# Hybrid attention block: one reduction over two banks, the first bank's mask as a product, transposes one slot later

## Chip, cores, metric

One core of a Trainium2 chip. The metric is the device time of one execution in microseconds.

## What is computed

An input of 8 sequences of 256 tokens with 128 channels goes through four layers, each as `x = x + layer(layernorm(x))`: a differential attention, a feed forward, a causal linear attention, and the same feed forward again. The change is in the first of them. Cut to what matters:

```
Q, K, V = (X @ W).reshape(B, N, 16, 16)          # 16 heads, 2 maps of width 8 in each
A1 = where(causal, Q1 K1^T / sqrt(8), -inf)
A2 = where(causal, Q2 K2^T / sqrt(8), -inf)
attn = softmax(A1) - lam * softmax(A2)
O = attn @ V
O = O / rms(O) * rms_scale * 0.2
x = x + O @ Wo
```

So each sequence has 32 maps of 256 x 256 scores with a causal mask, 256 maps in all, and the softmax subtracts the maximum of each row.

## The kernel before

The program has a first block (projections to Q and K, split into three bf16 parts each, and the composed weights of the feed forward) and a second one that holds the attention and all that follows. Every engine's order is written out by hand: a loop over *slots*, and in each slot each engine takes the piece of work that belongs to it, of units at different ages. Semaphores tie the engines together.

A *unit* is four maps; there are 64 units, four to a *group* of 16 maps, eight to a sequence. In its own slot a unit is scored (lag 0). Query rows 0 to 127 can only see keys 0 to 127, so their four maps of 128 x 128 fit in PSUM bank 0 (`S_BANK`, L1002). Query rows 128 to 255 see all 256 keys; they take banks 1 and 2, two maps of 128 x 256 in each (L1007). There is one set of these three banks, so a unit's scores wait until the unit before has had its row maxima taken from the same bank (`scores_wait`, semaphore `maxed`). The future keys are masked in two ways. In banks 1 and 2 PE adds a product of a bf16 identity and a bf16 matrix of -1e30 above the diagonal, 256 columns for each bank (`score_masks`, L1015), at the end of the slot's scores. In bank 0 VectorE does it: one instruction for each of the four maps adds the matrix `future` and takes the row maximum (L948), with an accumulator read after each. Banks 1 and 2 get one reduction each (L953). The maxima go to `rowmax`.

The rest of a unit's life, as lags in slots behind its scoring (L71, L72):

- 4 (`L_SHIFT`), once for a group: PE transposes `rowmax` (L1105), ScalarE makes the high part of the shift (L898), VectorE the low part (L914), and SP writes both as rows next to the queries (`store_shift`, L736).
- 6 (`L_EXP`): PE computes the scores once more, transposed and with the shift in them (L1039, L1044), into banks 3 and 4; ScalarE takes the exponentials (L824), GpSimd zeroes the future (L776). This is interleaved with the scores of the current unit in `both`.
- 8 (`L_PV`): PE multiplies with the values (L1081, L1085, bank 5 or 6), ScalarE copies the result (L842).
- 9 (`L_OT`): PE transposes it (L1127, bank 7), ScalarE copies it (L851).

Once for a sequence, counted from its first unit, follow the reciprocal of the denominators (16, VectorE L972), products and difference on GpSimd (16, 17), squares and their sum (19, ScalarE L868, VectorE L932), the inverse root (20), GpSimd's normalisation (21, L757), the transposes of the normalised output into bank 7 (`L_OPT` 21, L1139) with ScalarE's copy (L887), the output projection (`L_OPROJ` 22, L1157) with VectorE's residual (L923), and the statistics for the next layer norm (`L_STAT` 22, L281 to L289). The transposes of a sequence thus stand on PE at the end of slots 5, 13, 21 and so on, and the projection in the slot after.

In each slot PE's order is: bank 0 of the current unit with the first third of the shifted scores; values; rowmax transposes or the output projection where due; banks 1 and 2 with the other shifted scores; masks (L1015); output transposes (L1127); transposes of the normalised output (L1139) where due. VectorE's order is: bank 0's maxima; low part of the shift and residual where due; bank 1's; mean squares where due; bank 2's; reciprocal; statistics.

## Time and profile before

| | |
|---|---|
| median of 3 runs | 455.25 us (454.56 to 455.97) |
| profiled execution | 455.39 us |
| its span, first to last instruction | 453.3 us |
| mean granted TensorE clock | 0.944 |
| PE busy | 386.5 us, 85% |
| VectorE (DVE) busy | 293.9 us, 65% |
| ScalarE (ACT) busy | 257.0 us, 57% |
| GpSimd (POOL) busy | 203.2 us, 45% |

Shares of the span are averages over stages: the first block lasts to about 90 us, the scoring of the 64 units from 94 to 280 us, the end of the attention to about 300 us, and then come the feed forward, the linear attention and the second feed forward. In the rows, PE is a product, PEld the load of its stationary operand, and a time in brackets is how long the engine stood idle before the row and what ended that. Rows of the same line that follow closely are merged, with their number behind an x.

### The profile page before, as it was taken

How to read it: one execution, taken by the hardware profiler on the slowest of the kernel's cores; microseconds unless marked ns; L12 is line 12 of the kernel's file. 1: busy time of each engine (PE TensorE's matmuls, PEld its weight loads, DVE VectorE, ACT ScalarE, POOL GpSimd, SP SyncE). 2: the span in 40 equal slices, each digit the busy share in tenths (PEclk: the TensorE clock that was granted, in tenths of full speed). 3: DMA queues.
4: the chain of work that ended last, by engine and by line, in shares of the span. 5: the costliest groups of instructions: out<-in, count | busy, mean ns of one | idle time of the engine just before them, and what ended most of it. 6: DMA issues, size and time to landing. Idle time of an engine off the chain costs nothing.

```text
span 453.3 us, 10148 instructions
## 1 busy us (share of the span) xinstructions
PE 386.5 (85%) x3380; PEld 244.5 (54%) x3380; DVE 293.9 (65%) x1019; ACT 257.0 (57%) x631; POOL 203.2 (45%) x324
## 2 busy tenths in 40 slices
PE   0799689769999888979799798888688999999996
PEld 0566479623455544545455454444475666555674
DVE  6576454169899797989989797110142789999201
ACT  3333134203688777877878686847667433444832
POOL 5223224001558475675848485733001788773000
PEclk9999799955899999999999999956999999999999
DMA  8889969953555434242544400000000000000011
GB/s 205 251 269 309 260 143 235 217 86 46 81 82 82 74 60 76 36 89 35 87 59 75 72 3 3 4 1 0 0 2 1 1 0 2 0 0 2 0 48 46
DMA packets 47347, 34.51 MB, mean 76 GB/s; under 512 B 20032, under 2 KB 41664, under 8 KB 47296
## 3 DMA queue, kind: packets, MB, share of 16 engines
q1 hardware_dynamic: 47296, 33.86, 35.8%
q8 instruction: 28, 0.46, 0.5%
q14 instruction: 23, 0.19, 0.2%
HBM read 25.20 MB, written 8.39 MB: 74 GB/s over the span
## 4 chain that ended last, share of the span: by engine, by line
PE 31%; DVE 26%; issue 9%; ACT 8%; POOL 4%; DMA 1%; DVEq 0%; POOLq 0%; SPq 0%
DVE ps L948 7%; DVE arena L953 7%; PE ps L1258 5%; PE ps L1249 3%; PE ps L1081 3%; PE ps L1461 3%; PE ps L1007 3%; DVE arena L1392 3%; DVE arena L948 2%; PE ps L1157 2%; ACT arena L1202 2%; ACT arena L824 2%; POOL arena L757 2%; PE ps L1002 2%; DVE arena L1405 2%
## 5 line engine op out<-in xcount | busy, mean ns | idle before, releaser
L776 POOL TENSOR_SCALAR_AFFINE_SELECT arena<-arena 128x256 f32<-128x256 f32 (+1 forms) x192 | 90.3, 482 | 97.8 <-ACT arena L824 93.8
L824 ACT ACTIVATE arena<-ps 128x512 f32<-128x512 f32 x192 | 109.5, 604 | 26.0 <-PE ps L1039 25.5
L953 DVE TENSOR_REDUCE arena<-ps 128x2 f32<-128x512 f32 x128 | 82.9, 686 | 6.5 <-PE ps L1015 6.0
L948 DVE CUSTOM_DVE_ANT_0 ps<-ps,future 128x128 f32<-128x128 f32 x256 | 66.4, 321 | 11.9 <-PE ps L1002 11.5
L1039 PE MATMUL ps<-stacks 50*128 50x256 bf16 x256 | 51.4, 281 | 1.2 <-ACT arena L824 1.1
L1333 POOL TENSOR_TENSOR arena<-arena 128x1024 f32<-128x1024 f32 x16 | 34.2, 2134 | 32.6 <-DVE arena L1418 32.1
L1007 PE MATMUL ps<-stacks 48*128 48x256 bf16 x256 | 45.5, 288 | 0.9 <-ACT arena L824 0.5
L391 POOL TENSOR_TENSOR qk_parts_sb<-qk_rest,qk_parts_sb 128x512 bf16<-128x512 f32 x16 | 19.1, 1209 | 51.2 <-DVE qk_parts_sb L491 51.2
L1081 PE MATMUL ps<-arena 128*17 128x256 f32 x512 | 41.4, 396 | 0.0
L1002 PE MATMUL ps<-stacks 48*128 48x128 bf16 x256 | 26.7, 228 | 16.8 <-DVE ps L906 6.1
L948 DVE DVE_READ_ACCUMULATOR2_ANT arena<- 128x1 f32 x256 | 36.3, 142 | 0.0
L1461 PE MATMUL ps<-arena,upto 128*128 128x384 f32 x96 | 36.0, 487 | 0.0
L1002 PEld LDWEIGHTS ps<-stacks 48*128 48x128 bf16 x256 | 15.7, 98 | 31.1 <-issue 17.6
L1258 PE MATMUL ps<-w,arena 128*128 128x128 f32 x256 | 30.3, 276 | 1.8 <-ACT arena L1225 1.3
L1258 PEld LDWEIGHTS ps<-w,arena 128*128 128x128 f32 x256 | 29.3, 192 | 3.8 <-ACT arena L1225 2.0
L1249 PE MATMUL ps<-arena,w 128*128 128x512 f32 x64 | 30.6, 627 | 0.3 <-DVE arena L1392 0.3
L1007 PEld LDWEIGHTS ps<-stacks 48*128 48x128 bf16 x256 | 17.8, 96 | 22.6 <-issue 10.7
L1231 DVE TENSOR_TENSOR xs<-ps,xs 128x512 f32<-128x512 f32 x8 | 5.5, 690 | 34.1 <-PE ps L1258 34.1
L1127 PE MATMUL ps<-ident,arena 128*128 128x128 f32 x128 | 26.3, 288 | 1.4 <-issue 0.6
L1015 PE MATMUL ps<-future_bf,ident_bf 128*128 128x256 bf16 x128 | 26.8, 294 | 0.0
L1085 PE MATMUL ps<-arena 128*17 128x128 f32 x512 | 26.4, 279 | 0.0
L1044 PE MATMUL ps<-stacks 50*128 50x128 bf16 x256 | 25.6, 222 | 0.0
(129 smaller groups left out, 750.6 us busy)
## 6 DMA issues: line engine op xcount, KB each, us to landing
stacks<-qk_parts SPq DMA_DIRECT2D x96, 128.0 KB, 4.6
qk_parts<-qk_parts_sb SPq DMA_DIRECT2D x16, 384.0 KB, 4.1
arena<-in_L_ffn_fc_B_dram SPq DMA_DIRECT2D x4, 1024.0 KB, 7.3
arena<-in_L_ffn_fc_A_dram SPq DMA_DIRECT2D x16, 256.0 KB, 4.7
xs<-in_L_attn_a_X_dram SPq DMA_DIRECT2D x4, 256.0 KB, 4.0
qk_parts<-qk_parts_sb SPq DMA_DIRECT2D x8, 128.0 KB, 4.4
stacks<-arena SPq DMA_DIRECT2D x64, 4.0 KB
out_dram<-xs SPq DMA_DIRECT2D x4, 256.0 KB, 2.3
```

The costliest lines, as they stand in the source:

```text
L776: nc.gpsimd.affine_select(out=diag, in_=diag, compare_op=ALU.is_ge, fill=0.0, base=0, pattern=[[0, 2 if s < 2 else UMAPS], [1, P]], channe ...
L824: nc.scalar.activation(probs[:, r, s, :], ps[:, bank, :], ACT.Exp, scale=SCALE).then_inc(exp_done, 1)
L948: last = nc.vector.tensor_tensor_reduce(out=block, in0=block, in1=future[:], scale=1.0, scalar=LOWEST, op0=ALU.add, op1=ALU.max, accum_out ...
L953: last = nc.vector.tensor_reduce(out=rowmax[:, gs, 1, at:at + 2], in_=ps[:, bank, :].rearrange("p (m k) -> p m k", m=2), axis=AX, op=ALU.max)
L1002: last = nc.tensor.matmul(bank[:, m * P:(m + 1) * P], q[:, m0 + m, 0:P], k[:, m0 + m, 0:P], start=True, stop=True)
L1007: nc.tensor.matmul(bank[:, m * SEQ:(m + 1) * SEQ], q[:, m0 + 2 * s - 2 + m, P:SEQ], k[:, m0 + 2 * s - 2 + m, :], start=(m == 0), stop=Fals ...
L1039: last = nc.tensor.matmul(bank[:, m * SEQ:(m + 1) * SEQ], k[:, m0 + 2 * s + m, 0:P], q[:, m0 + 2 * s + m, :], start=True, stop=True)
L1081: nc.tensor.matmul(ps[32 * m:32 * m + DV + 1, O_BANK + r, 0:SEQ], vaug[:, v, 0, head, :], probs[:, p, m // 2, m % 2 * SEQ:m % 2 * SEQ + SE ...
L1249: nc.tensor.matmul(ps[:, 2 + c, :], w1[:, c * P:(c + 1) * P], f_xnT[:, k % 2, :], start=True, stop=True).then_inc(S["up"], 1)
L1258: last = nc.tensor.matmul(ps[:, 6 + k % 2, t * D:(t + 1) * D], hT[:, k % 2, c, t * P:(t + 1) * P], w2[:, c, :], start=(c == 0), stop=(c == ...
L1333: nc.gpsimd.tensor_tensor(kv[:, w, t, 0:DH, :].rearrange("p e (h d) -> p e h d", d=DH), kh.unsqueeze(1).to_broadcast([P, DH, HEADS, DH]), ...
L1461: last = nc.tensor.matmul(bank, upto[:], rows, start=True, stop=(t == 0))
```

## The change

Bank 0 is masked as the other two are: `score_masks` gets a third product, of 512 columns, ahead of the two of 256, so bank 0's scores are left open (`stop=False`) and its semaphore count comes from that product. VectorE takes one reduction over bank 0 (four maps) and one over banks 1 and 2 together (four maps); the second waits for all three banks and counts two on `maxed`. `future` goes, and `future_bf` holds four copies. The transposes of the normalised output, the output projection and the statistics come one slot later each. In the diff, `...` marks what is left out.

```
-L_DEN, L_DIFF, L_SQ, L_MS, L_ROOT, L_NORM, L_OPT, L_OPROJ, L_STAT = 16, 17, 19, 19, 20, 21, 21, 22, 22
+L_DEN, L_DIFF, L_SQ, L_MS, L_ROOT, L_NORM, L_OPT, L_OPROJ, L_STAT = 16, 17, 19, 19, 20, 21, 22, 23, 23
...
-                nc.gpsimd.memset(future[:], 0.0)
...
-                                        base=0, pattern=[[0, 2], [-1, P]], channel_multiplier=1)
-                nc.gpsimd.affine_select(out=future[:], in_=future[:], compare_op=ALU.is_ge, fill=NEG,
-                                        base=0, pattern=[[-1, P]], channel_multiplier=1).then_inc(consts, 1)
+                                        base=0, pattern=[[0, UMAPS], [-1, P]], channel_multiplier=1)\
+                    .then_inc(consts, 1)
...
-                    for s in range(BANKS_U):
-                        bank = S_BANK + s
-                        dve.wait_ge(scored, BANKS_U * n + s + 1)
-                        if s == 0:
-
-                            carry_wait(dve, tick_dve)
-                            for m in range(UMAPS):
-                                block = ps[:, bank, m * P:(m + 1) * P]
-                                at = UMAPS * uu + m
-                                last = nc.vector.tensor_tensor_reduce(
-                                    out=block, in0=block, in1=future[:], scale=1.0, scalar=LOWEST, op0=ALU.add,
-                                    op1=ALU.max, accum_out=rowmax[:, gs, 0, at:at + 1])
-                        else:
-                            at = UMAPS * uu + 2 * s - 2
-                            last = nc.vector.tensor_reduce(
-                                out=rowmax[:, gs, 1, at:at + 2], in_=ps[:, bank, :].rearrange("p (m k) -> p m k", m=2),
-                                axis=AX, op=ALU.max)
-                        last.then_inc(maxed, 1)
-                        if s == 0:
-                            shift_low(it, j)
-                            residual(it, j)
-                        if s == 1:
-                            mean_squares(it, j)
+                    dve.wait_ge(scored, BANKS_U * n + 1)
+                    nc.vector.tensor_reduce(
+                        out=rowmax[:, gs, 0, UMAPS * uu:UMAPS * (uu + 1)],
+                        in_=ps[:, S_BANK, :].rearrange("p (m k) -> p m k", m=UMAPS),
+                        axis=AX, op=ALU.max).then_inc(maxed, 1)
+                    shift_low(it, j)
+                    residual(it, j)
+                    dve.wait_ge(scored, BANKS_U * (n + 1))
+                    nc.vector.tensor_reduce(
+                        out=rowmax[:, gs, 1, UMAPS * uu:UMAPS * (uu + 1)],
+                        in_=ps[:, S_BANK + 1:S_BANK + 3, :].rearrange("p b (m k) -> p (b m) k", m=2),
+                        axis=AX, op=ALU.max).then_inc(maxed, 2)
+                    mean_squares(it, j)
...
-                    last = nc.tensor.matmul(bank[:, m * P:(m + 1) * P], q[:, m0 + m, 0:P],
-                                            k[:, m0 + m, 0:P], start=True, stop=True)
-                    if m == UMAPS - 1:
-                        last.then_inc(scored, 1)
+                    nc.tensor.matmul(bank[:, m * P:(m + 1) * P], q[:, m0 + m, 0:P],
+                                     k[:, m0 + m, 0:P], start=(m == 0), stop=False, skip_group_check=True)
...
+                    nc.tensor.matmul(ps[:, S_BANK, :], ident_bf[:], future_bf[:].rearrange("p m k -> p (m k)"),
+                                     start=False, stop=True, skip_group_check=True).then_inc(scored, 1)
```

The order on PE from the scores of bank 2 to the next unit's bank 0, in a plain slot. Before (L1007 scores of banks 1 and 2, L1044 shifted scores, L1015 masks, L1127 output transposes, L1002 scores of bank 0):

```order
L1007 MATMUL ps<-stacks 128x256 [waits exp_done,maxed]
L1044 MATMUL ps<-stacks 128x128
L1007 MATMUL ps<-stacks 128x256
L1044 MATMUL ps<-stacks 128x128 x3
L1015 MATMUL ps<-future_bf,ident_bf 128x2x128 x2
L1127 MATMUL ps<-ident,arena 128x128 [waits o_copied,ot_copied]
L1127 MATMUL ps<-ident,arena 128x128
L1002 MATMUL ps<-stacks 128x128 [waits exp_done,maxed]
```

and with the change, where the same lines are L992, L1031, L1002, L1114 and L989, and L998 is the new mask:

```order
L992 MATMUL ps<-stacks 128x256 [waits exp_done,maxed]
L1031 MATMUL ps<-stacks 128x128
L992 MATMUL ps<-stacks 128x256
L1031 MATMUL ps<-stacks 128x128 x3
L998 MATMUL ps<-future_bf,ident_bf 128x512
L1002 MATMUL ps<-future_bf,ident_bf 128x2x128 x2
L1114 MATMUL ps<-ident,arena 128x128 [waits o_copied,ot_copied]
L1114 MATMUL ps<-ident,arena 128x128
L989 MATMUL ps<-stacks 128x128 [waits exp_done,maxed]
```

The last writer of bank 0 now stands four instructions ahead of the next unit's first scores in it, where before it stood at the slot's beginning.

VectorE in a slot with a shift, before (L948 masked maxima, named ISA, with the reads of the accumulator; L914 low part of the shift):

```order
L948 ISA ps,arena<-ps,future 128x128
L948 ISA arena 128x1
L914 SCALAR_TENSOR_TENSOR arena<-ps,arena 16x256
L953 TENSOR_REDUCE arena<-ps 128x2 x2
L972 RECIPROCAL arena<-arena 128x64
```

and now (L937 bank 0, L911 the low part, L944 banks 1 and 2, L959 the reciprocal):

```order
L937 TENSOR_REDUCE arena<-ps 128x4 [waits scored]
L911 SCALAR_TENSOR_TENSOR arena<-ps,arena 16x256 [waits shift_hi]
L944 TENSOR_REDUCE arena<-ps 128x4 [waits scored]
L959 RECIPROCAL arena<-arena 128x64 [waits post,o_copied]
L937 TENSOR_REDUCE arena<-ps 128x4 [waits scored]
L944 TENSOR_REDUCE arena<-ps 128x4 [waits scored]
```

The low part keeps its place behind bank 0's maximum, which itself now follows the mask product.

PE around the transposes of the normalised output, before (L1139 the transposes, L1157 the projection of the next slot):

```order
L1127 MATMUL ps<-ident,arena 128x128
L1139 MATMUL ps<-ident,arena 128x128 [waits resid_done,o_copied,normed]
L1139 MATMUL ps<-ident,arena 128x128 x3
L1002 MATMUL ps<-stacks 128x128 [waits exp_done,shift_in20,maxed]
L1039 MATMUL ps<-stacks 128x256
```

and now (L1126 the transposes, L1144 the projection):

```order
L1114 MATMUL ps<-ident,arena 128x128
L1126 MATMUL ps<-ident,arena 128x128 [waits resid_done,o_copied,normed]
L1126 MATMUL ps<-ident,arena 128x128 x3
L989 MATMUL ps<-stacks 128x128 [waits exp_done,maxed]
L1026 MATMUL ps<-stacks 128x256
```

The neighbours are the same; the whole piece stands one slot later, so that the scores behind it wait for no shift rows.

## Rows read from the trace of the kernel before

**Rows 1.** The page, part 4: shares of the chain that ended last
```profile
PE 31%; DVE 26%; issue 9%; ACT 8%; POOL 4%; DMA 1%; DVEq 0%; POOLq 0%; SPq 0%
```

**Rows 2.** Stretches: stretch, its us, busy PE, PEld, DVE, ACT, POOL, PEclk, DMA
```profile
94.00:114.00 20.00, 18.22 (x98) 6.85 (x98) 18.04 (x81) 4.24 (x8) 2.18 (x5) 0.50 0.47 70
...
118.00:276.00 158.00, 137.66 (x2003) 80.14 (x1998) 138.37 (x587) 124.24 (x310) 102.43 (x191) 1.00 0.41 64
...
292.00:304.00 12.00, 10.12 (x80) 5.58 (x80) 0.69 (x1) 7.61 (x25) 5.83 (x12) 0.59 0.01 1
```

**Rows 3.** Timeline, a plain slot: start us, us, engine, line, operation
```profile
212.20 0.23 PE L1002 MATMUL ps<-stacks 48*128 48x128 bf16 x1
...
213.30 0.28 PE L1007 MATMUL ps<-stacks 48*128 48x256 bf16 x1
...
213.39 0.27 DVE L948 CUSTOM_DVE_ANT_0 ps<-ps,future 128x128 f32<-128x128 f32 x1
...
213.85 0.39 PE L1015 MATMUL ps<-future_bf,ident_bf 128*128 128x256 bf16 x2
...
214.32 1.28 DVE L953 TENSOR_REDUCE arena<-ps 128x2 f32<-128x512 f32 x2
214.52 0.23 PE L1002 MATMUL ps<-stacks 48*128 48x128 bf16 x1
```

**Rows 4.** Timeline, a slot with rowmax transposes, ahead of rows 3
```profile
209.44 0.21 PE L1002 MATMUL ps<-stacks 48*128 48x128 bf16 x1 [0.80 <-DVE arena L948]
...
210.85 0.28 PE L1007 MATMUL ps<-stacks 48*128 48x256 bf16 x1
...
211.36 0.41 DVE L914 SCALAR_TENSOR_TENSOR arena<-ps,arena 16x256 bf16<-16x256 f32 x1
...
211.83 0.44 PE L1127 MATMUL ps<-ident,arena 128*128 128x128 f32 x2
```

**Rows 5.** Timeline, the end of slot 37 and slot 38 to its bank 1
```profile
200.28 0.39 PE L1015 MATMUL ps<-future_bf,ident_bf 128*128 128x256 bf16 x2
...
200.60 1.29 DVE L953 TENSOR_REDUCE arena<-ps 128x2 f32<-128x512 f32 x2 [0.35 <-PE ps L1015]
...
201.29 0.30 ACT L851 COPY arena<-ps 128x136 f32<-128x136 f32 x1
...
202.31 0.66 PE L1139 MATMUL ps<-ident,arena 128*128 128x128 f32 x4 [1.42 <-POOL arena L757]
...
202.90 0.23 PE L1002 MATMUL ps<-stacks 48*128 48x128 bf16 x1
...
205.09 0.28 PE L1007 MATMUL ps<-stacks 48*128 48x256 bf16 x1
```

**Rows 6.** Timeline, PE: first scores of units 24, 46, 56 and 63
```profile
159.80 0.21 PE L1002 MATMUL ps<-stacks 48*128 48x128 bf16 x1 [0.80 <-DVE arena L948]
...
227.20 0.23 PE L1002 MATMUL ps<-stacks 48*128 48x128 bf16 x1
...
258.04 0.21 PE L1002 MATMUL ps<-stacks 48*128 48x128 bf16 x1 [0.80 <-DVE arena L948]
...
279.16 0.21 PE L1002 MATMUL ps<-stacks 48*128 48x128 bf16 x1
```

**Rows 7.** The page, part 5: the masked maxima
```profile
L948 DVE CUSTOM_DVE_ANT_0 ps<-ps,future 128x128 f32<-128x128 f32 x256 | 66.4, 321 | 11.9 <-PE ps L1002 11.5
```

**Rows 8.** One line, L1405: durations ns min/median/max, first and last start, forms
```profile
L1405 DVE TENSOR_REDUCE arena<-arena x16: 1353/1353/1354, 357.5 to 416.9; 128x144 f32<-128x1152 f32 x16
```

**Rows 9.** Timeline, units 4 and 8 (last row), at the low clock
```profile
105.33 1.03 PE L1007 MATMUL ps<-stacks 48*128 48x256 bf16 x4
...
106.29 0.61 PE L1015 MATMUL ps<-future_bf,ident_bf 128*128 128x256 bf16 x2
...
106.72 1.29 DVE L953 TENSOR_REDUCE arena<-ps 128x2 f32<-128x512 f32 x2 [0.47 <-PE ps L1015]
...
117.14 0.39 PE L1015 MATMUL ps<-future_bf,ident_bf 128*128 128x256 bf16 x2
```

More of the change, by code:

```diff
@@ L112, in hybrid_kernel @@
         ident_bf = sb("ident_bf", [P, P], BF16)
-        future = sb("future", [P, P])
-        future_bf = sb("future_bf", [P, 2, P], BF16)
+        future_bf = sb("future_bf", [P, UMAPS, P], BF16)
         upto = sb("upto", [P, P])
@@ L1015, in score_masks @@
                         nc.tensor.matmul(bank.rearrange("p (m k) -> p m k", m=2)[:, :, P:SEQ], ident_bf[:],
-                                         future_bf[:], start=False, stop=True,
+                                         future_bf[:, 0:2], start=False, stop=True,
                                          skip_group_check=True).then_inc(scored, 1)
```

## The prediction

> **What bounds the kernel now.** I read the chain of waits first [rows 1]: no engine carries most of it, so the stages have to be looked at one by one. The table of stretches [rows 2] shows that the change falls into one stretch, 94 to 280 us, in which the 64 units of four maps are scored. From 118 to 276 us PE is busy 137.7 of 158 us and VectorE 138.4: two engines in balance, and neither wait is long. In the timeline of a plain slot [rows 3] the slot begins at 212.20 and the next at 214.52, so it takes 2.3 us. In it VectorE's four masked maxima take 0.93 (213.39 to 214.32) and the two reductions 1.28, together 2.2. What matters is how they interlock. Bank 0's maxima run while PE weighs values and scores banks 1 and 2; the reductions of banks 1 and 2 run while PE does its masks, its transposes and the next unit's bank 0. The slot is full on both engines and neither waits for a round trip.
>
> From here m is the start of a slot's first mask product (L1015), B the start of its bank 0 scores (L1002), b the start of its bank 1 scores (L1007). A plain slot [rows 3]: B to b 1.10 (212.20 to 213.30), b to m 0.55, m to the next B 0.67 or less.
>
> The other slots of a sequence (eight slots) carry extras: a slot with rowmax transposes has B to b 1.41, 0.31 more, and VectorE's low half of the shift (L914, 0.41) [rows 4]; one waits for GpSimd's normalisation before its transposes, which start 2.03 after m at 202.31, and the next has the output projection, B to b 2.19 (202.90 to 205.09) [rows 5]. Eight slots repeat in 24.30 us (202.90 [rows 5] to 227.20 [rows 6]).
>
> **The change part by part.** *VectorE.* Off go 4 masked maxima a unit, 256 of 321 ns with their 256 accumulator reads [rows 7]; one reduction of 512 elements comes, 0.69 as L953's. Two reductions of 512 become one of 1024. No row has it; the nearest is L1405's, 1152 elements in 1353 ns from SBUF [rows 8]. Between 0.69 for 512 and 1.35 for 1152 it is 1.04 ns an element, so 1.22 us; bounds 1.15 and 1.40. VectorE's plain slot falls from 2.2 to 0.60 (the spacing of back-to-back reductions: 1.28 less 0.69) and 1.22, 1.8 us. Alone that would be a gain of 0.4 us a slot.
>
> *PE.* One product of 512 columns a unit. Two of 256 columns (L1015) take 0.39 together where one (L1007) takes 0.28 [rows 3], so 256 columns are 0.11 and 512 are 0.22. The Trainium skill, "TensorE: Matmul & The Clock Gate", section "Back-to-back issue gap", gives some 131 ns for a product of 512 columns in a stream of weight loads and products; by it the sum below would be 0.09 times 64, some 6 us, smaller. Nothing below uses it.
>
> *The wait that comes.* Bank 0 is now complete only after this mask, which PE issues at the end of the slot, and the next thing that PE wants after masks and output transposes is the same bank 0 (it waits for the maximum of it). So mask, maximum, next scores are one after another, and everything behind is queued: values, banks 1 and 2, and again the mask. Its length: mask to reduction is 0.32 for 256 columns (200.28 to 200.60 [rows 5]), 0.11 more for 512, 0.43; the reduction 0.69; VectorE to PE 0.06 (L914 ends 211.77, L1127 starts 211.83 [rows 4]). Next B = m + 1.18, where PE would be free at about 0.67 + 0.22. The wide reduction ends at m + 0.43 + 0.60 + 1.22 = m + 2.25, so b = m + 2.31, PE itself being there at 2.28. Then 0.55 to the next mask: **a plain slot takes 2.86 instead of 2.3.**
>
> *Slots with extras.* The low half of the shift and the residual (VectorE 0.41, 0.42) stand behind the bank 0 reduction, and PE waits for each before its output transposes: it ends at m + 0.43 + 0.60 + 0.41 = 1.44, transposes at 1.50, next B 0.35 later at m + 1.85 (211.83 to 212.20 is 0.37 [rows 4]). Such a slot takes 1.85 + 1.10 + 0.55 = 3.50. Into a slot with rowmax transposes: 2.31 + 0.31 + 0.55 = 3.17; out of the projection's slot and into one of these: 1.85 + 1.41 + 0.55 = 3.81. *The later transposes* gain: normalisation is done by then, and what they wait for is ScalarE's copy of the output transposes (L851 ends 1.31 after m [rows 5], 1.45 with what precedes it now); with 0.59 to B it is m + 2.04, where before it was 2.62. But the projection's 2.19 follows: 2.04 + 2.19 + 0.55 = 4.78. Mean squares, reciprocal and statistics on VectorE fall into its new idle time and cost nothing; if the slot became short again they would be back on the chain, some 2.2 us a sequence. GpSimd loses a memset and a select in the first block, under DMA: nothing. SP's queue keeps its order. A shift's rows land up to 3.2 us after the low half; now PE comes for them 3.2 us after it as well, so 0 to 0.3 us 14 times: 0 taken, 4 in the range.
>
> *Sum.* A sequence: 3 x 2.86 + 3.17 + 2 x 3.50 + 4.78 + 3.81 = 27.34, against 24.30: 3 us each.
> - Units 0 to 8 run at half clock (granted 0.50 in 94 to 114 us [rows 2]): mask to reduction 0.43 (106.29 to 106.72) and 0.21 for the columns, 1.82, 0.06, b to m 0.96 [rows 9], 3.48 against a plain 2.3: 8 slots, 9.4, with the extras of units 4 and 8 **10**.
> - From unit 8's mask (117.14 [rows 9]) to unit 24 (159.80 [rows 6]) 42.66 now; then 4 x 3.50 + 7 x 2.86 + 3 x 3.17 + 4.78 + 1.85 = 50.16: **7.5**.
> - Units 24 to 56, 159.80 to 258.04 [rows 6], 98.24 now; 4 x 27.34 = 109.4: **11.1**.
> - Units 56 to 63, 21.12 now (to 279.16 [rows 6]); 1.41 + 0.55 + 2 x 3.50 + 3 x 2.86 + 3.17 + 2.04 = 22.75: **1.6**.
> - The last projection, 1.08, moves behind unit 63: **1.1**. After it the order of the tail is as before: nothing.
>
> Together 31.3 us. The profiled execution took 455.39 us (0.14 above the median of 455.25): 486.7, **487 us**.
>
> **The rivals.** *Faster: PE is the bound.* If the round trip from mask to next B cost no more than PE's own work (0.22 + 0.67), VectorE's relief would show: eight slots of 2.30 + 0.22, two times 0.31, 1.08 for the projection and 0.59 for the transposes, 22.5 us a sequence, 1.8 less, some 14 us in all: 441 us. For it: VectorE and PE are both nearly full now, and the 1.4 us wait of the later transposes really goes. Against: the reduction alone is 0.69, and both waits are in the program. The sign turns where the round trip is 0.38 shorter than 1.18, that is a reduction of 0.3 us. Chance 5 in 100.
> *No difference*, the two effects cancelling within 0.3%, about what a measurement of this kernel can tell from no change: the round trip would be 0.8 long. 2 in 100.
> *The clock stays low.* The granted clock was 0.50 (1.2 GHz) up to 114 us while PE was busy 18.2 of 20 us in the records, was 1.00 from 118 on, and fell again, to a mean of 0.59, in 292 to 304 us when PE was thinner [rows 2]. With 0.3 to 0.9 us of waiting in every slot PE may be granted 1.2 GHz later, or lose 2.4 GHz between. At half clock a slot has 0.64 + 0.69 + 0.06 to B, up to twice 1.10 to b and 0.96 to m, 4.55 instead of 2.86: if the rise comes 16 slots later that is 27 us (514 us), if never, in some 55 slots, 93 (580 us). Against: now waits of 1.42 us [rows 5] come in each sequence and 118 to 276 us has 1.00 throughout. The same page of the Trainium skill, Part 1, says that the low clock is the default and activity releases it; by it this case is the likelier the thinner PE's work becomes. Chance 10 in 100.
> *The change does less than it says*: the reduction over two banks costs two instructions' time. 1.29 for 1.22 delays b by 0.07: 4 us, inside the range.
>
> **How the numbers follow.** My forecast has 83 in 100 and is itself slower. Its bounds: every step of the loop 0.1 shorter is 6 us less; the mask at half its price 6; a clock that rises a few units sooner 3. Upwards: the wide reduction at 1.40, 0.18 in some 50 slots, 9; the shift's rows 4; clock up a few slots later 5. Not all at once: 477 to 500, and into the clock's case up to 506. Slower 0.93, same 0.02, faster 0.05.
>
> **What would show it.** Right: slots of 2.86 and 3.50, a sequence of 27 us; PE idle before L989 some 0.3 to 0.9 us in nearly every slot, put down to VectorE's L937; VectorE busy some 60 us less, with over 0.8 us idle before L937 in a slot; L1126 no longer waiting for GpSimd but for ScalarE's copy, if anything. Wrong: L989 starting within 0.9 us after L998, slots of 2.5 us, or a clock row of 0.50 beyond 135 us.

## The result, and the profile after

The changed kernel takes 483.64 us, the median of 4 runs (481.34 to 485.84), beside 455.61 (454.56 to 459.62) for the kernel before: a ratio of 1.060 (95% interval 1.055 to 1.065), 28.0 us more. 487 was forecast. Ratios, here and below, leave out executions more than 1.5% above the fastest of the same kernel, which ran at a lower clock; medians and ranges hold all of them. Its profiled execution took 483.22 us, with a span of 481.5 and a mean granted clock of 0.946.

The page of the changed kernel: busy times, shares of the chain that ended last, and the groups (busy us, mean ns | idle before, what ended it).

```profile
PE 395.7 (82%) x3444; PEld 250.1 (52%) x3444; DVE 264.0 (55%) x507; ACT 261.5 (54%) x631; POOL 203.6 (42%) x322
...
PE 48%; DVE 14%; issue 9%; ACT 7%; POOL 2%; DVEq 0%; POOLq 0%
...
L937 DVE TENSOR_REDUCE arena<-ps 128x4 f32<-128x512 f32 x64 | 44.3, 692 | 87.8 <-PE ps L998 87.8
L944 DVE TENSOR_REDUCE arena<-ps 128x4 f32<-128x1024 f32 x64 | 77.5, 1212 | 0.0
...
L989 PE MATMUL ps<-stacks 48*128 48x128 bf16 x256 | 27.3, 232 | 22.5 <-DVE arena L937 11.6
...
L1114 PE MATMUL ps<-ident,arena 128*128 128x128 f32 x128 | 26.0, 285 | 18.3 <-DVE arena L911 11.9
```

VectorE is busy 30 us less than before and now stands idle 87.8 us ahead of bank 0's maximum, all of it for the mask product L998. PE waits in its turn for that maximum (L989) and for the low part of the shift behind it (L1114). The chain's share of VectorE fell from 26% [rows 1] to 14%, though the kernel got slower: the chain now goes through PE, the mask and back. By the page alone VectorE would seem to have been relieved and PE to have become the bound. The slots tell more.

Timeline of the changed kernel, two plain slots.

```profile
239.66 0.23 PE L989 MATMUL ps<-stacks 48*128 48x128 bf16 x1 [0.35 <-DVE arena L937]
...
240.79 0.28 PE L992 MATMUL ps<-stacks 48*128 48x256 bf16 x1
...
241.34 0.39 PE L998 MATMUL ps<-future_bf,ident_bf 128*128 128x512 bf16 x1
...
241.77 0.69 DVE L937 TENSOR_REDUCE arena<-ps 128x4 f32<-128x512 f32 x1 [1.03 <-PE ps L998]
...
242.38 1.22 DVE L944 TENSOR_REDUCE arena<-ps 128x4 f32<-128x1024 f32 x1
...
242.52 0.23 PE L989 MATMUL ps<-stacks 48*128 48x128 bf16 x1 [0.35 <-DVE arena L937]
...
243.65 0.28 PE L992 MATMUL ps<-stacks 48*128 48x256 bf16 x1
```

The loop reads off directly: mask product at 241.34, reduction 0.43 later, 0.69 long, the next bank 0 scores 0.06 behind its end, at 242.52. B to b is 1.13, b to m 0.55 (the prediction's letters: m the first mask, B bank 0's scores, b bank 1's). A plain slot takes 2.86 us, where [rows 3] have 2.3.

A slot that has the low part of the shift, from its mask to the next slot's start, same view:

```profile
234.97 0.39 PE L998 MATMUL ps<-future_bf,ident_bf 128*128 128x512 bf16 x1
...
235.40 0.69 DVE L937 TENSOR_REDUCE arena<-ps 128x4 f32<-128x512 f32 x1 [0.71 <-PE ps L998]
...
236.00 0.40 DVE L911 SCALAR_TENSOR_TENSOR arena<-ps,arena 16x256 bf16<-16x256 f32 x1
...
236.46 0.44 PE L1114 MATMUL ps<-ident,arena 128*128 128x128 f32 x2 [0.89 <-DVE arena L911]
...
236.83 0.23 PE L989 MATMUL ps<-stacks 48*128 48x128 bf16 x1
```

From mask to the next B it is 1.86 here, and PE stands 0.89 us before its output transposes.

The starts of units 0, 8, 24, 32, 40, 56 and 63 in the changed kernel, same view:

```profile
94.26 0.61 PE L989 MATMUL ps<-stacks 48*128 48x128 bf16 x4 [7.38 <-DVE ps L903]
...
122.37 0.26 PE L989 MATMUL ps<-stacks 48*128 48x128 bf16 x1 [0.40 <-issue]
...
178.11 0.23 PE L989 MATMUL ps<-stacks 48*128 48x128 bf16 x1
...
205.56 0.23 PE L989 MATMUL ps<-stacks 48*128 48x128 bf16 x1
...
233.00 0.23 PE L989 MATMUL ps<-stacks 48*128 48x128 bf16 x1
...
288.57 0.23 PE L989 MATMUL ps<-stacks 48*128 48x128 bf16 x1
...
311.39 0.23 PE L989 MATMUL ps<-stacks 48*128 48x128 bf16 x1
```

Before, unit 0 started at 94.69, 0.4 us later, and unit 8 at 114.09. The kernel before reaches unit 24 at 159.80 [rows 6], so 18.3 us are lost by then. Units 24 to 56 take 110.46 against 98.24, 12.2 more; units 56 to 63 22.82 against 21.12, 1.7 more. A sequence is 27.44 (205.56 to 233.00); the next one is 28.12, by one slot of 3.52 for 2.82, and the two around them 27.45. What follows unit 63's start is 4.0 us shorter: 481.5 less 311.39 is 170.1, and 453.3 less 279.16 [rows 6] is 174.1. With unit 0's start that makes 28.2 us of span.

Stretches of the changed kernel (us, busy PE, PEld, DVE, ACT, POOL, then the granted clock):

```profile
94.00:134.00 40.00, 32.44 (x216) 14.53 (x217) 19.13 (x24) 10.01 (x21) 6.20 (x13) 0.52 0.34 52
134.00:320.00 186.00, 152.81 (x2111) 88.55 (x2108) 116.64 (x171) 133.83 (x319) 104.40 (x194) 1.00 0.34 51
320.00:334.00 14.00, 11.59 (x142) 5.82 (x144) 1.35 (x4) 12.04 (x36) 11.38 (x20) 1.00 0.01 3
```

The clock rose only behind 132 us (granted 0.50 in 130 to 132, 0.91 in 132 to 134), where before it stood at 1.00 from 118 on [rows 2]. Behind unit 63 it was the other way: 2.4 GHz nearly throughout (mean 0.99 from 312 to 481 us), where before it was granted 0.59 between 292 and 304 us [rows 2] and 0.95 from 280 to 453.

### The profile page after: what moved, and what is told of

It is laid out like the page before. It is cut to its first block, busy times and chain, and to the rows that moved or that the text cites. A ratio compares the mean times of both kernels' runs of the same rounds, so it can differ in the third digit from the quotient of the medians.

```text
span 481.5 us, 9761 instructions
## 1 busy us (share of the span) xinstructions
PE 395.7 (82%) x3444; PEld 250.1 (52%) x3444; DVE 264.0 (55%) x507; ACT 261.5 (54%) x631; POOL 203.6 (42%) x322
## 4 chain that ended last, share of the span: by engine, by line
PE 48%; DVE 14%; issue 9%; ACT 7%; POOL 2%; DVEq 0%; POOLq 0%
PE ps L1068 7%; PE ps L992 7%; PE ps L1245 5%; PE ps L998 5%; DVE arena L937 5%; PE ps L989 3%; PE ps L1448 3%; PE ps L1072 3%; DVE arena L1379 2%; PE ps L1114 2%; PE ps L1236 2%; ACT arena L1189 2%; DVE arena L944 2%; PE ps L1026 2%; DVE arena L1392 1%
## 5 line engine op out<-in xcount | busy, mean ns | idle before, releaser
L773 POOL TENSOR_SCALAR_AFFINE_SELECT arena<-arena 128x256 f32<-128x256 f32 (+1 forms) x192 | 90.6, 482 | 125.8 <-ACT arena L821 121.5
L821 ACT ACTIVATE arena<-ps 128x512 f32<-128x512 f32 x192 | 107.9, 597 | 43.2 <-PE ps L1026 41.0
L937 DVE TENSOR_REDUCE arena<-ps 128x4 f32<-128x512 f32 x64 | 44.3, 692 | 87.8 <-PE ps L998 87.8
L944 DVE TENSOR_REDUCE arena<-ps 128x4 f32<-128x1024 f32 x64 | 77.5, 1212 | 0.0
L992 PE MATMUL ps<-stacks 48*128 48x256 bf16 x256 | 43.4, 293 | 3.5 <-DVE arena L944 3.5
L989 PE MATMUL ps<-stacks 48*128 48x128 bf16 x256 | 27.3, 232 | 22.5 <-DVE arena L937 11.6
L1114 PE MATMUL ps<-ident,arena 128*128 128x128 f32 x128 | 26.0, 285 | 18.3 <-DVE arena L911 11.9
L989 PEld LDWEIGHTS ps<-stacks 48*128 48x128 bf16 x256 | 15.6, 99 | 37.9 <-DVE arena L937 19.7
L1245 PE MATMUL ps<-w,arena 128*128 128x128 f32 x256 | 31.9, 286 | 1.8 <-ACT arena L1212 1.3
L1245 PEld LDWEIGHTS ps<-w,arena 128*128 128x128 f32 x256 | 30.9, 201 | 3.8 <-ACT arena L1212 2.0
L992 PEld LDWEIGHTS ps<-stacks 48*128 48x128 bf16 x256 | 20.1, 99 | 20.9 <-DVE arena L944 9.6
L1236 PE MATMUL ps<-arena,w 128*128 128x512 f32 x64 | 28.8, 595 | 0.3 <-DVE arena L1379 0.3
L1114 PEld LDWEIGHTS ps<-ident,arena 128*128 128x128 f32 x128 | 14.8, 142 | 25.1 <-DVE arena L911 15.7
L998 PE MATMUL ps<-future_bf,ident_bf 128*128 128x512 bf16 x64 | 27.1, 424 | 0.0
L1002 PE MATMUL ps<-future_bf,ident_bf 128*128 128x256 bf16 x128 | 26.9, 296 | 0.0
L1031 PE MATMUL ps<-stacks 50*128 50x128 bf16 x256 | 25.6, 222 | 0.0
```

The source lines that it names most:

```text
L773: nc.gpsimd.affine_select(out=diag, in_=diag, compare_op=ALU.is_ge, fill=0.0, base=0, pattern=[[0, 2 if s < 2 else UMAPS], [1, P]], channe ...
L821: nc.scalar.activation(probs[:, r, s, :], ps[:, bank, :], ACT.Exp, scale=SCALE).then_inc(exp_done, 1)
L937: nc.vector.tensor_reduce(out=rowmax[:, gs, 0, UMAPS * uu:UMAPS * (uu + 1)], in_=ps[:, S_BANK, :].rearrange("p (m k) -> p m k", m=UMAPS), ...
L944: nc.vector.tensor_reduce(out=rowmax[:, gs, 1, UMAPS * uu:UMAPS * (uu + 1)], in_=ps[:, S_BANK + 1:S_BANK + 3, :].rearrange("p b (m k) -> p ...
L989: nc.tensor.matmul(bank[:, m * P:(m + 1) * P], q[:, m0 + m, 0:P], k[:, m0 + m, 0:P], start=(m == 0), stop=False, skip_group_check=True)
L992: nc.tensor.matmul(bank[:, m * SEQ:(m + 1) * SEQ], q[:, m0 + 2 * s - 2 + m, P:SEQ], k[:, m0 + 2 * s - 2 + m, :], start=(m == 0), stop=Fals ...
```

## The experiments

The kernel before ran beside each set, at medians of 456.55 (e3 to e6), 457.54 (e1, e2, e7, e8) and 455.65 us (f1 to f4); ratios are to it, with 95% intervals. In the edits `...` marks what is left out. Since the end of the program moves with the clock, the one profiled execution of each is also cut at first scores, in us: the start of unit 0, four stretches between starts of units, from unit 63's start to the end (after), and from unit 0 to 63. It is one execution each, and a spell at the low clock falls where it falls: two of f1's sequences between units 24 and 56 are 24.8 long and the other two 23.3, which alone is 3 us.

| | start | units 0-8 | 8-24 | 24-56 | 56-63 | after | 0 to 63 |
|---|---|---|---|---|---|---|---|
| before | 94.7 | 19.4 | 45.7 | 98.2 | 21.1 | 174.1 | 184.5 |
| changed | 94.3 | 28.1 | 55.7 | 110.5 | 22.8 | 170.1 | 217.1 |
| e3 | 92.4 | 23.9 | 47.8 | 99.8 | 21.2 | 169.9 | 192.7 |
| e6 | 92.6 | 31.5 | 58.5 | 115.9 | 24.1 | 174.2 | 230.0 |
| e4 | 92.6 | 26.4 | 52.5 | 107.3 | 22.2 | 170.7 | 208.3 |
| e5 | 90.6 | 28.1 | 54.9 | 112.4 | 25.2 | 172.2 | 220.6 |
| e1 | 93.3 | 19.4 | 44.8 | 96.4 | 20.8 | 170.0 | 181.4 |
| e2 | 93.7 | 23.2 | 47.8 | 99.7 | 21.3 | 177.3 | 192.0 |
| e7 | 94.8 | 23.2 | 45.0 | 96.6 | 20.3 | 170.2 | 185.1 |
| f1 | 94.2 | 16.5 | 45.5 | 96.2 | 19.9 | 168.9 | 178.0 |
| f2 | 96.1 | 21.4 | 47.8 | 100.3 | 22.1 | 171.8 | 191.6 |
| f3 | 93.4 | 16.5 | 45.9 | 93.7 | 20.0 | 168.8 | 176.0 |
| f4 | 95.7 | 16.5 | 43.5 | 91.9 | 19.6 | 168.9 | 171.5 |

Three kernels first take the change apart at its suspected place: the round trip through bank 0.

**e3_mask_early.** The same product, issued right behind bank 0's scores.

```
-                    nc.tensor.matmul(ps[:, S_BANK, :], ident_bf[:], future_bf[:]...).then_inc(scored, 1)   # in score_masks
+                    nc.tensor.matmul(ps[:, S_BANK, :], ident_bf[:], future_bf[:]...).then_inc(scored, 1)   # in both(), after bank 0
```

> The changed kernel with one move: bank 0's mask product stands right behind bank 0's scores at the slot's beginning, and not at its end. Same work on every engine. Theory (the round trip mask, maximum, next scores at the slot's end is what costs): the maximum now runs beside the values, PE waits for it no longer, a plain slot falls from 2.86 to 2.45 to 2.5 us, a sequence from 27.4 to about 23, and the kernel takes 446 us (440 to 452), less than before the change. Rival A (the product's own time on PE, or the wide reduction, costs): nothing is gained, 478 to 486 us.

Measured: 458.75 us (456.56 to 462.5), ratio 1.009 [1.004, 1.014]. Moving one instruction takes back 24.9 of the 28 us, so the loss is a matter of where the product stands. But 446 was expected and it did not go below the kernel before: that half missed. Timeline of this kernel, a plain slot:

```profile
219.88 0.21 PE L989 MATMUL ps<-stacks 48*128 48x128 bf16 x1
...
220.89 0.68 DVE L937 TENSOR_REDUCE arena<-ps 128x4 f32<-128x512 f32 x1
...
221.30 0.28 PE L992 MATMUL ps<-stacks 48*128 48x256 bf16 x1
...
221.74 1.08 ACT L821 ACTIVATE arena<-ps 128x512 f32<-128x512 f32 x2 [0.57 <-PE ps L1024]
...
221.85 0.39 PE L1000 MATMUL ps<-future_bf,ident_bf 128*128 128x256 bf16 x2
...
222.48 0.21 PE L989 MATMUL ps<-stacks 48*128 48x128 bf16 x1
```

No wait stands before L989, and the slot still takes 2.60. B to b is 1.42 for 1.10 [rows 3], b to m 0.55 as there, m to B 0.63: here the product costs PE 0.32 us and not the 0.22 that it adds between the masks. PE's own order fills the slot, but f3 below shows that a second loop gives the same 2.60.

**e6_mask_last.** Bank 0's product behind the two others, and its maximum waits for all three.

```
-                    dve.wait_ge(scored, BANKS_U * n + 1)
+                    dve.wait_ge(scored, BANKS_U * (n + 1))
```

> The changed kernel with the three masks in the other order: banks 1 and 2 first, bank 0 last, and the bank 0 maximum waits for all three. Same work, but bank 0 is complete 0.22 us later. Theory: every slot gets 0.2 us longer, 64 slots, 12 to 14 us: 496 us (492 to 500). Rival A: the product costs the same wherever it stands among the masks, so 482 to 486 us.

Measured: 498.06 us (494.89 to 502.52), ratio 1.091 [1.081, 1.102]: 14.4 us over the changed kernel, as expected. Some 13 of it are in units 0 to 63; what follows is 4 us longer and unit 0 starts 1.7 earlier, so the nearness of 14.4 to 64 times 0.22 is in part chance. Timeline, end of a plain slot:

```profile
189.67 0.23 PE L989 MATMUL ps<-stacks 48*128 48x128 bf16 x1 [0.57 <-DVE arena L937]
...
191.35 0.39 PE L1000 MATMUL ps<-future_bf,ident_bf 128*128 128x256 bf16 x2
...
192.00 0.69 DVE L937 TENSOR_REDUCE arena<-ps 128x4 f32<-128x512 f32 x1 [1.25 <-PE ps L1000]
...
192.75 0.23 PE L989 MATMUL ps<-stacks 48*128 48x128 bf16 x1 [0.57 <-DVE arena L937]
```

The slot grew from 2.86 to 3.08, the 0.22 by which the mask is later: the loop from mask to maximum to scores is closed. In a steady sequence seven slots of eight grow by that much, and the one with the late transposes stays at 3.75. The amount of work is the changed kernel's own.

**e4_no_product.** The product is dropped, and bank 0's count comes from bank 1's mask, so the wait stays. Row maxima of bank 0 are taken over all of its keys.

```
-                    nc.tensor.matmul(ps[:, S_BANK, :], ident_bf[:], future_bf[:]...).then_inc(scored, 1)
...
-                                          skip_group_check=True).then_inc(scored, 1)
+                                          skip_group_check=True).then_inc(scored, s)
```

> The changed kernel without the product of 512 columns; the count for bank 0 comes from the first of the two masks that remain, so the maximum still starts at the slot's end. Bank 0's mask is left out of the row maxima. Theory: only 0.11 to 0.2 us a slot is saved (PE's columns, and the maximum starts 0.32 after the first mask instead of 0.43), so 472 to 477 us, still some 20 us slower than before the change. Rival A (the product's own time): back to 455 to 462 us.

Measured: 475.7 us (473.36 to 477.19), ratio 1.046 [1.036, 1.056], as expected: 7.9 us back, and the other 20 stay as long as the wait stays where it is. Timeline, a plain slot from its mask:

```profile
203.55 0.39 PE L1000 MATMUL ps<-future_bf,ident_bf 128*128 128x256 bf16 x2
...
203.88 0.69 DVE L937 TENSOR_REDUCE arena<-ps 128x4 f32<-128x512 f32 x1 [0.81 <-PE ps L1000]
...
204.62 0.23 PE L989 MATMUL ps<-stacks 48*128 48x128 bf16 x1 [0.46 <-DVE arena L937]
```

Even the 7.9 is not the product's own time on PE, which still waits 0.46 before the scores. It is the maximum, which starts 0.33 behind the mask and not 0.43; a plain slot is 2.72.

**e5_transposes_back.** The changed kernel with the transposes where they were.

```
-... L_OPT, L_OPROJ, L_STAT = 16, 17, 19, 19, 20, 21, 22, 23, 23
+... L_OPT, L_OPROJ, L_STAT = 16, 17, 19, 19, 20, 21, 21, 22, 22
```

> The changed kernel with the transposes, the projection and the statistics back in their old slots (21, 22, 22). Theory: PE waits for GpSimd's normalisation again, which ends about 2.1 us after the first mask of the slot where ScalarE's copy ends at 1.4: 0.6 to 0.7 us a sequence, 4 to 6 us, 488 to 490 us. Rival B (the later transposes are what costs): 470 us or less.

Measured: 490.7 us (485.2 to 495.0), ratio 1.069 [1.056, 1.082], 7.1 us over the changed kernel by the medians, but only 3.2 by the executions that the ratio rests on (485.2 and 488.4), and 3.5 in units 0 to 63 (a sequence 28.10 for 27.45); 4 to 6 were expected. Timeline:

```profile
221.76 0.66 PE L1126 MATMUL ps<-ident,arena 128*128 128x128 f32 x4 [1.30 <-POOL arena L754]
```

The wait for GpSimd's normalisation, as in [rows 5], is back: 20.5 us in all before L1126, where the changed kernel has 1.8 and the kernel before 21.3.

**e1_later_only.** The kernel before with nothing but the later lags: the same line, the other way.

> The kernel before with one part of the change: transposes, projection and statistics one slot later. Theory: PE waits for ScalarE's copy instead of GpSimd's normalisation, 0.65 us less for each of 8 sequences, and nothing new stands in the way since bank 0's maxima still run at the slot's beginning: 450 us (448 to 454). Rival B (the later pieces collide with something else): 455 or more.

Measured: 448.27 us (445.56 to 453.09), ratio 0.989 [0.981, 0.997]. The median is 9.3 us under that of before, yet units 0 to 63 are only 3.1 us shorter (181.4 for 184.5), and a sequence is 24.10 for 24.30. Much of the rest stands in the clock: before's own 17 runs of this set go from 449.42 us at a mean clock of 0.962 to 462.45 at 0.922, and e1's from 445.56 at 0.958. At like clocks (before 450.19 at 0.958) it is 4.6. The ratio says some 5 us. So by its own waits this part gains 0.65 us a steady sequence with the new masking (e5) but only 0.20 with the old; the rest of the 3.1 comes from single longer slots of the kernel before, one of them 3.46 for 2.3. In these profiles the stretch after unit 63 is another 2 to 4 shorter (174.1 to 170.0 here, 172.2 to 170.1 from e5 to the changed kernel).

**e2_wide_only.** The kernel before with one reduction over banks 1 and 2 and the mean squares behind it, masked maxima kept.

```
-                        dve.wait_ge(scored, BANKS_U * n + s + 1)
...
+                    dve.wait_ge(scored, BANKS_U * (n + 1))
+                    nc.vector.tensor_reduce(
+                        out=rowmax[:, gs, 1, UMAPS * uu:UMAPS * (uu + 1)],
+                        in_=ps[:, S_BANK + 1:S_BANK + 3, :].rearrange("p b (m k) -> p (b m) k", m=2),
+                        axis=AX, op=ALU.max).then_inc(maxed, 2)
```

> The kernel before with one part of the change: one reduction over banks 1 and 2 instead of two, bank 0 with VectorE's masked maxima as before. Theory: VectorE is relieved of some 0.06 us a slot, and bank 1's maximum is known 0.5 us later, which PE does not miss because the values stand between: no difference, 455 us (453 to 458). Rival C (the later count for bank 1 holds PE): 460 or more.

Measured: 465.32 us (463.48 to 467.4), ratio 1.028 [1.022, 1.035]. The expectation missed by 10 us, and rival C's 460 or more came. Timeline, a slot at the low clock:

```profile
98.61 0.60 PE L996 MATMUL ps<-stacks 48*128 48x128 bf16 x4
98.80 1.23 DVE L951 TENSOR_REDUCE arena<-ps 128x4 f32<-128x1024 f32 x1 [0.73 <-PE ps L1009]
...
100.08 1.03 PE L1001 MATMUL ps<-stacks 48*128 48x256 bf16 x4 [0.86 <-DVE arena L951]
...
101.04 0.61 PE L1009 MATMUL ps<-future_bf,ident_bf 128*128 128x256 bf16 x2
...
101.58 0.61 PE L996 MATMUL ps<-stacks 48*128 48x128 bf16 x4
```

The wide reduction makes a loop of its own: it starts only after bank 2's mask, and holds bank 1 until its end. Scores 0.96, mask to its start 0.73, 1.23 and 0.05 make 2.97 a slot, where the kernel before needs 2.3. From unit 0 to unit 8 that is 23.2 us against 19.4. Units 0 to 63 lose 7.5 in all, and 3.1 are lost behind them, where the clock was 0.65 from 300 to 330 us. All six runs had a mean clock of 0.919 to 0.930, so this goes with the edit; by what path isn't shown.

So far: e3 shows the round trip, but also that without it the masks on PE gain nothing over e1, which keeps them on VectorE (192.7 against 181.4 us for units 0 to 63). The next six look for what holds the slot when VectorE does not.

**e7_early_no_product.** e3 without the product; bank 0's mask is left out of the row maxima.

```
-                        nc.tensor.matmul(ps[:, S_BANK, :], ident_bf[:], future_bf[:]...).then_inc(scored, 1)   # in both()
...
+                    if m == UMAPS - 1:
+                        last.then_inc(scored, 1)
```

> The kernel with the early mask of bank 0 (458.75 us), without that product: bank 0's mask is left out of the row maxima, and the maximum follows the scores. Its timeline shows a plain slot of 2.60, in which scores and product take 0.64 where the scores alone took 0.32. Theory (once the round trip is gone PE's own work is the bound, and the product costs 0.3 us of it): a plain slot of 2.28, 64 x 0.3 = 20 us less, 440 us (436 to 446). Rival D (ScalarE or another engine is the bound at 2.5 us a slot): 452 or more.

Measured: 451.33 us (447.83 to 453.4), ratio 0.995 [0.990, 1.000]: 7.4 us under e3, well short of what was expected. It is also e4 with bank 0's count raised by its last scores and not by the mask at the slot's end, the same work for PE and VectorE: 475.7 to 451.3, and 208.3 to 185.1 for units 0 to 63. That is the round trip by itself. The plain slots stop at 2.3 to 2.4, though VectorE has 0.4 us a slot less to do than before and PE as much. Against e1, which has the same lags and VectorE's masks, units 24 to 56 take 96.6 for 96.4: relieving VectorE gains nothing there (a steady sequence is 23.70 for 24.10, but two of the four are 24.6).

**e8_no_masks.** As e7, and banks 1 and 2 without masks in the row maxima too (the exponentials are still masked, so the shift is a maximum over all keys, and the softmax divides it out).

```
-                for s in range(1, BANKS_U):
-                    nc.tensor.matmul(bank..., ident_bf[:], future_bf[:, 0:2], ...).then_inc(scored, 1)
+                return
```

> As the one before, and also without the masks of banks 1 and 2 in the row maxima. The shift is then the maximum over all keys, which the softmax cancels; the exponentials are masked afterwards as always. Theory: PE's slot loses 0.22 to 0.33 more and falls to 2.0, and ScalarE, whose three exponentials and two copies take some 2.3 us a slot, becomes the bound: a gain of at most 0.1 us a slot in plain slots and the full one in the others, 433 us (427 to 440). Rival E (PE's waits between slots stay): the same time as without bank 0's product.

Measured: 448.27 us (443.67 to 454.29), ratio 0.988 [0.980, 0.996]; missed by 15 us. The two masks are gone from PE, some 0.22 a slot, and plain slots are still 2.30. (Its profiled execution took 454.29, 6 above the median, so it isn't in the table.)

**f1_no_masks_two.** e8 with the two separate reductions of the kernel before.

> The kernel without masks in the row maxima (448.27 us), with one reduction each for banks 1 and 2 again instead of the wide one. Theory (the wide reduction makes a round trip of its own while the clock is low: in units 2 to 8 of the wide-reduction kernel a slot takes 2.97 us instead of 2.3): those slots shrink, 3 to 6 us less, 444 us (440 to 447). Rival: the wide reduction is not at fault there, no change, 448 or more.

Measured: 445.76 us (442.0 to 447.9), ratio 0.978 [0.972, 0.984], 2.5 us under e8 and inside what was expected, though the two intervals overlap. The slots are clearer: at the low clock plain ones fall to 1.80, and units 0 to 8 take 16.5 us for e8's 19.3, the wide reduction's price again.

**f2_early_two.** e3 with the two separate reductions; all masks kept.

> The kernel with bank 0's mask product behind bank 0's scores (458.75 us), with one reduction each for banks 1 and 2. Theory: the units at the low clock lose 0.5 us each, 4 to 6 us, 453 us (450 to 456); the later slots stay at 2.60, which PE's own work sets. Rival: 458 or more.

Measured: 458.59 us (456.67 to 461.94), ratio 1.009 [1.005, 1.013], as e3: missed. Units 0 to 8 are 2.5 us shorter, but units 24 to 63 1.4 and what follows 2.0 longer. The wide reduction is thus not what keeps e3 above e1 at the full clock; the product's 0.32 is, as e7 shows.

**f3_copy_on_dve.** f1 with the copy of the weighted values moved from ScalarE to VectorE.

```
-                    nc.scalar.copy(ot_sb[:, r, :], ps[:, O_BANK + r, 0:SEQ]).then_inc(ot_copied, 1)
+                    nc.vector.tensor_copy(ot_sb[:, r, :], ps[:, O_BANK + r, 0:SEQ]).then_inc(ot_copied, 1)
```

> The first kernel of this group with the copy of the weighted values (0.38 us a slot) moved from ScalarE to VectorE, which has the time now. It tells apart why plain slots stop at 2.30 whatever VectorE and PE are spared. Theory F (a round trip: the second exponential 0.60, 0.15 to PE's next bank 0 scores, 1.10 to the scores of bank 1, 0.44 to the next second exponential, 2.29 in all): the copy is not on it, no gain, within 3 us of the first kernel. Rival G (ScalarE's throughput, 2.0 to 2.3 us of work a slot): 10 to 15 us less.

Measured: 438.55 us (436.39 to 439.94), ratio 0.962 [0.957, 0.967], 7.2 us under f1: between the 3 at most of theory F and the 10 to 15 of rival G, so the time decides nothing and the slots have to. Timeline, a plain slot:

```profile
208.01 0.21 PE L991 MATMUL ps<-stacks 48*128 48x128 bf16 x1 [0.22 <-ACT arena L821]
...
209.11 0.28 PE L996 MATMUL ps<-stacks 48*128 48x256 bf16 x1
...
209.57 1.08 ACT L821 ACTIVATE arena<-ps 128x512 f32<-128x512 f32 x2 [0.47 <-PE ps L1024]
...
210.31 0.21 PE L991 MATMUL ps<-stacks 48*128 48x128 bf16 x1 [0.22 <-ACT arena L821]
```

PE and ScalarE both have gaps, so neither is full, and ScalarE has 0.4 us a slot less to do than in f1; still it takes 2.30. The legs of theory F's round trip add up to it: the first exponential of the pair (209.57) runs 0.60, to 210.17, and frees the bank that the next slot writes first; PE starts 0.14 later; B to b is 1.10; 0.46 after b the next pair starts. 0.60 + 0.14 + 1.10 + 0.46 = 2.30. e3's slot fits it too: 0.60 + 0.14 + 1.42 + 0.44 = 2.60. Its product stood between B and b, a leg of this loop as well as a part of PE's own work, so e3 alone cannot tell the two apart. The 7.2 us did not come from the slots: a steady sequence is 23.4 here and 23.3 in f1 (the slot with the late transposes 3.58 for 4.13, but others longer). The profiled executions differ by 2.9, of which 2.5 between units 24 and 56, where the clock was 1.00 from 156 to 250 us here and 0.96 in f1, which has slots of 4.5 to 5.0 in there. The rest is in executions without a profile: f3's six had mean clocks of 0.952 to 0.959, f1's 0.931 to 0.953, and f1's two at 0.950 and 0.953 took 442.85 and 442.0. So the clock explains the better part, and some 3 us at like clocks stay open.

**f4_split_values.** f1, with the second half of the values' products moved behind bank 1's scores, which shortens B to b.

```
-                    for t in range(TPS):
-                        weigh_values(it, j, t)
+                    weigh_values(it, j, 0)
...
+                if live(unit(it, j, L_PV), UNITS):
+                    weigh_values(it, j, 1)
```

> The first kernel of this group with the products with the values split on PE: the first half (L1081's) stays ahead of the scores of bank 1, the second half (L1085's) goes behind them. The same work. Theory F: the round trip of the second exponential loses the second half, 0.2 to 0.33 us, plain slots fall from 2.30 to 2.05 and the slots with more ScalarE work gain less: 8 to 15 us less than the first kernel, 434 us (429 to 440). Rival G (ScalarE's throughput): less than 3 us.

Measured: 437.98 us (435.13 to 445.96), ratio 0.959 [0.954, 0.965], 7.8 us under f1, inside the expected range, but much of it clock as in f3. Timeline:

```profile
206.58 0.23 PE L991 MATMUL ps<-stacks 48*128 48x128 bf16 x1
...
207.27 1.94 ACT L821 ACTIVATE arena<-ps 128x512 f32<-128x512 f32 x3
...
207.46 0.28 PE L996 MATMUL ps<-stacks 48*128 48x256 bf16 x1
...
208.82 0.23 PE L991 MATMUL ps<-stacks 48*128 48x128 bf16 x1
```

B to b is 0.88, 0.22 shorter, and with the same work slots at last fall below 2.30, to 2.25: together with f3, where less work for ScalarE left them at 2.30, this makes the round trip the limit. 2.05 was expected. The slot did not fall by the whole 0.22, since ScalarE's three exponentials now follow one another without a gap. A steady sequence is 22.97 for f1's 23.27, so of the 4.3 us between units 24 and 56 (91.9 for 96.2) only 1.2 are the slots'; 3.1 are f1's two sequences with low clock.

## Why the prediction was right, and where it was off

**The round trip** was the forecast's main step and held to the hundredth: mask to reduction 0.43, reduction 0.69, VectorE to PE 0.06, a plain slot 2.86. e3 (the product moved away: 24.9 us back), e6 (0.22 later: 14.4 more), e4 (the product gone, the wait left: 7.9 back) and e7 (the wait gone as well: another 24) tie it to the wait and not to the work. The product itself took 0.23 us among the masks (241.34 to 241.57, where the next mask starts) for 0.22 forecast. From mask to mask, as the forecast counts them, the slots with extras were 3.19 (3.17 forecast), 3.51 (3.50), 4.74 (4.78) and 3.86 (3.81); a sequence 27.44 for 27.34; units 24 to 56 cost 12.2 for 11.1; units 56 to 63 1.7 for 1.6.

**The wide reduction** took 1.21 us for the 1.22 between [rows 3] and [rows 8]. In the changed kernel its end sets b, which the sum had. What it costs by itself, a loop of its own at the low clock, the sum did not need; e2 and f1 show it.

**The low-clock units**: forecast 10 to unit 8 and 7.5 from there to unit 24, 17.5; measured 8.7 and 10.0, 18.7. A plain slot at the low clock took 3.49 for 3.48 forecast. The clock rose behind 132 us, in slot 10, and not at unit 8; slots 8 and 9 took 4.8 and 4.3 us (122.37, 127.21 and 131.53 are the starts of units 8 to 10), which is near the 4.55 of the rival. The range had this upwards ("clock up a few slots later"); it is a small piece of the rival *the clock stays low*, whose other slots did not come.

**The later transposes** were to shorten m to B from 2.62 to 2.04, 0.58 a sequence or some 4 us in seven sequences. It measured 2.00, and against e5 the gain is 0.65 a sequence and 3.5 us in units 0 to 63: the step held. In the kernel before the same move gives 0.20 a sequence (e1).

**The tail** is the term with the wrong sign: +1.1 forecast, -4.0 measured. The working took the clock there as given. From unit 63's start to the end the mean granted clock was 0.95 before, 0.99 in the changed kernel, 0.98 in e1, 0.97 in e5, 0.95 in e6 and 0.93 in e2, and the stretch took 174.1, 170.1, 170.0, 172.2, 174.2 and 177.3 us: it goes with the clock. The moved projection's +1.1 is not to be seen beside that; e6, which has it, is as long as before at the same clock. What decides the clock there stays open. The table shows 4.1 us of the same kind in e1 and 2.1 between e5 and the changed kernel, so the later transposes may have a part in it; e6, which has them too, has 174.2, so they don't decide it alone. With the units' 32.7 us for the 30.2 forecast and unit 0's start 0.4 earlier this gives the 28.2 for 31.3: two misses of 2.5 and 5.1 in opposite directions, so that the sum came within 3.4 us of the time is in part luck.

**VectorE's relief** was told in two ways that do not agree. The working has 0.4 us a slot, which is 26 in 64 slots; among the signs stands "some 60 us less". It was 30 (293.9 to 264.0). The sum does not use it. The other signs came: 0.35 us of waiting for L937 before a plain slot's scores, 1.4 idle before L937 in a slot, and GpSimd's part of the wait before the transposes down from 21.3 us to 1.8.

**The rival that PE is the bound (441 us)** was priced wrongly, and more so than its 5 in 100 tells. Its condition was made true in e3, where the round trip costs less than PE's own work, and the time was 458.75. Two steps of it failed. The product costs PE 0.32 among the scores, not 0.22. And VectorE's relief of 0.4 a slot shows only in slots with its extras (3.42 for e1's 3.76 behind a sequence's projection): "two engines in balance" overlooked a third chain through ScalarE that stands at the same 2.3. Its legs are in the kernel before too, in its timeline behind [rows 3]:

```profile
213.74 1.09 ACT L824 ACTIVATE arena<-ps 128x512 f32<-128x512 f32 x2 [0.42 <-PE ps L1039]
...
214.52 0.23 PE L1002 MATMUL ps<-stacks 48*128 48x128 bf16 x1
...
215.62 0.28 PE L1007 MATMUL ps<-stacks 48*128 48x256 bf16 x1
...
216.06 1.08 ACT L824 ACTIVATE arena<-ps 128x512 f32<-128x512 f32 x2 [0.30 <-PE ps L1039]
```

ScalarE idles 0.42 and 0.30 before each pair, which reads like slack, and its busy share is 57%. But 213.74 + 0.60 ends the first one, B follows at 214.52, b 1.10 later, the next pair 0.44 after that: 2.32. In this slot VectorE is the last by a hair: its masked maxima end at 214.46, 0.06 before B, where ScalarE's end and its 0.14 would have allowed 214.48. PE's own work is 1.10 + 0.55 + 0.63 (e3's m to B, without a wait), 2.28. PE, VectorE and this loop all stood within 0.1 us of 2.3.

**Versions that beat both kernels.** With everything computed as before, e1 at 448.3 us, a gain of 1% (0.989 [0.981, 0.997]). With the row maxima over all keys, f4 at 438.0 and f3 at 438.6 us; these divide a different shift out of the softmax, which is safe only while future scores do not exceed the present ones by so much that the exponentials vanish. f3 and f4 together were not tried.

## What to carry over

When a mask, a copy or any last touch on a buffer moves to another engine, look not at what it costs but at how far its last writer then stands from the next user of the same buffer: at the end of a slot it put mask, maximum and next scores in a row, and the same instruction right behind the scores took 24.9 of the 28 us back. Before pricing the relief of an engine, close every loop through each buffer with a single copy, engines with gaps included, and add up its legs; where three of them stand at 2.3 us, freeing one gives next to nothing. Reductions merged over two banks save instructions and lengthen the time for which both banks are held.

## What was not expected of the hardware

- A 512-column bf16 product took 0.23 us of PE between the mask products and 0.32 between scores of 48 rows and values (e3: B to b 1.42 for 1.10).
- The granted clock goes with larger differences in this kernel than most single edits make. The unchanged kernel ran between 449.42 us (mean clock 0.962) and 463.73 (0.926), and f1 and f3, with steady sequences alike, differ by 7.2 us in their medians, some 3 at like clocks. Behind the scores PE was busy 10.1 of 12 us at 0.59 before [rows 2] and 11.6 of 14 at 1.00 after. Differences under 5 us are therefore better read from the slots than from the medians.
- VectorE began to read a bank 0.43 us after a 512-column mask product began and 0.32 after one of 256 columns [rows 5] (e4: 0.33); PE followed VectorE's end by 0.06 in every slot read.
